# Transposing by row halves of the array, and scores on its four quarters, in a fused Mamba and local-attention kernel

## The reference

```python
def local_attention(q, k, v):            # 8 heads of 64, windows of 64
    bq = q.reshape(b, h, w, WINDOW, d) * QK_SCALE
    ...                                  # keys and values: the window before and the own one
    sim = jnp.einsum('bhwid,bhwjd->bhwij', bq, bk)
    mask = (i < j) | (i > j + WINDOW) | (j == -1)
    sim = jnp.where(mask, -jnp.finfo(sim.dtype).max, sim)
    attn = jax.nn.softmax(sim, axis=-1)
    out = jnp.einsum('bhwij,bhwjd->bhwid', attn, bv)
```

## Time and profile before

| | |
|---|---|
| median of 3 runs | 1633.24 us (1629.99 to 1635.3) |
| the profiled execution's own time | 1627.94 us |
| its span, from first to last instruction | 1626.2 us |
| mean clock granted to TensorE, as a share of 2.4 GHz | 0.872 |
| PE busy | 1266.1 us, 8096 matmuls |
| PE weight loads busy (PEld) | 761.9 us, 8096 loads |
| DVE busy | 1111.9 us |
| ACT busy | 756.7 us |
| POOL busy | 729.8 us |

### The profile page before, as it was taken

The page is one execution under the profiler, slowest core; times in us unless marked ns, Lnnn a source line. Parts: engine busy times, 40 slices in busy tenths (PEclk is TensorE's granted clock), DMA queues, the critical chain, the costliest instruction groups (busy, mean ns, idle before and its releaser), DMA issues. The chain is left out here.

```text
span 1626.2 us, 22154 instructions
## 1 busy us (share of the span) xinstructions
PE 1266.1 (78%) x8096; PEld 761.9 (47%) x8096; DVE 1111.9 (68%) x1700; ACT 756.7 (47%) x1832; POOL 729.8 (45%) x357
## 2 busy tenths in 40 slices
PE   2867867887869888788879878798797878768685
PEld 0223433454545545445455545455464546455353
DVE  6859856968768667787686678686676755563442
ACT  1644525535545284443635365443655444444251
POOL 0007404655355634663455445464445545552351
PEclk8878978998989899888999889897998979889787
DMA  4000000000000000000000000000000000000000
GB/s 157 0 7 1 1 7 0 1 1 7 1 7 7 2 7 1 7 7 7 1 1 8 7 7 1 7 8 0 1 1 1 7 1 1 1 7 1 7 1 7
DMA packets 14317, 12.54 MB, mean 8 GB/s; under 512 B 1093, under 2 KB 12543, under 8 KB 14207
## 3 DMA queue, kind: packets, MB, share of 16 engines
q1 hardware_dynamic: 14207, 11.10, 2.2%
HBM read 9.00 MB, written 2.10 MB: 7 GB/s over the span
## 5 line engine op out<-in xcount | busy, mean ns | idle before, releaser
L805 DVE TENSOR_TENSOR_SCAN scan<-du,decay 128x1028 f32<-128x1028 f32 x128 | 392.0, 3079 | 68.6 <-ACT decay L593 68.5
L499 POOL TENSOR_TENSOR rn<-ssc,expo 128x16 f32<-128x16 f32 x64 | 186.1, 2908 | 457.2 <-DVE ssc L866 457.0
L995 PE MATMUL Y<-scan,diag 128*128 128x512 f32 x512 | 277.1, 669 | 77.6 <-DVE scan L805 77.6
L647 ACT ACTIVATE prob<-B,nmax 128x128 f32<-128x128 f32 x512 | 180.3, 377 | 326.6 <-DVE nmax L901 326.5
L519 POOL TENSOR_TENSOR qk<-qk,rn 128x1024 f32<-128x1024 f32 x64 | 199.2, 3113 | 5.0
L995 PEld LDWEIGHTS Y<-scan,diag 128*128 128x128 f32 x512 | 97.4, 210 | 186.8 <-DVE scan L805 107.4
L593 ACT ACTIVATE decay<-delta,negA 128x1024 f32<-128x1024 f32 x128 | 146.2, 1163 | 34.6 <-DVE scan L805 34.5
L610 ACT ACTIVATE sq<-A 128x512 f32<-128x512 f32 x128 | 74.6, 601 | 182.4 <-PE A L995 182.3
L515 POOL TENSOR_TENSOR qk<-qc,qs 128x1024 f32<-128x1024 f32 x64 | 153.8, 2404 | 2.5
L995 PE MATMUL B<-kT,qT 64*64 64x128 f32 x2048 | 151.4, 291 | 0.0
L995 PEld LDWEIGHTS B<-kT,qT 64*64 64x64 f32 x2048 | 117.9, 141 | 50.6 <-issue 50.6
(11 more groups left out here) (141 smaller groups left out, 2309.1 us busy)
## 6 DMA issues: line engine op xcount, KB each, us to landing
xT<-in_xT SPq DMA_DIRECT2D x8, 256.0 KB, 2.6
x<-in_x SPq DMA_DIRECT2D x8, 256.0 KB, 3.1
out<-outb SPq DMA_DIRECT2D x8, 256.0 KB, 2.3
wqkv<-in_wqkv SPq DMA_DIRECT2D x1, 1536.0 KB
w<-in_w SPq DMA_DIRECT2D x1, 682.0 KB
wo<-in_wo SPq DMA_DIRECT2D x1, 512.0 KB
bv<-in_bv SPq DMA_DIRECT2D x1, 328.0 KB, 3.9
rope_c<-in_rope_c SPq DMA_DIRECT2D x2, 128.0 KB
```

The source lines that it names most:

```text
L499: pool.tensor_tensor(rn[:, :], ssc[:, :], expo[:, 0:2 * HEADS], ALU.pow).then_inc(rn_sb, 1)
L647: ins = act.activation(prob[:, h, :], B[a][:, c * P:(c + 1) * P], ACT.Exp, bias=nmax[:, q % 2, h:h + 1], accum_out=den[:, q % 2, h:h + 1])
L805: dve.tensor_tensor_scan(state, step, a, 0.0, ALU.add, ALU.mult).then_inc(scan_sb, 1)
L995: return pe.matmul(dst, lhsT, rhs, start=start, stop=stop, skip_group_check=True)
```

## The change

Each of the three steps is laid out anew.

- Transposes work on 64 rows at a time: row half `w` (window `w`'s queries, or positions) has all 128 columns as its stationary operand and is moved through by a 64x64 piece of the identity, so that each transpose writes 64 columns. Row half 0 writes to `B[0]`, row half 1 to `B[1]`. There are 16 of them where there were 8, the two halves by turns, and both banks signal only at the end. `probs_T` therefore waits for the probabilities of all heads first, and `qk_T` for both copies of `probT`.
- `probT` is now laid out by window, and q and k lie together in one buffer, `qkT`, for one sequence instead of two. ACT still makes two copies of 128x512 for it, but each takes q and k of one window. The wait for the scores of the tile before (`s_ps`) stands where it was, ahead of the first copy.
- `scores` puts the mask in by four matmuls of 64 rows and 64 columns, one for each quarter of the array (row half `a`: even or odd heads; column half `w`: the window), and then goes through the pairs of heads with the four quarters by turns. Both signals come at the very end.

```diff
             def probs_T(q):
-                for a in range(2):
-                    pe.wait_ge(prob_sb, 2 * q + a + 1)
-                    for c in range(PAIRS):
-                        ins = pe.transpose(B[a][:, c * P:(c + 1) * P], prob[:, 2 * c + a, :], ident[:, :])
-                    ins.then_inc(pT_ps, 1)
+                pe.wait_ge(prob_sb, 2 * q + 2)
+                for h in range(HEADS):
+                    for w in range(2):
+                        ins = pe.transpose(B[w][:, h * WIN:(h + 1) * WIN], prob[half(w), h, :], ident[half(w), half(w)])
+                        if h == HEADS - 1:
+                            ins.then_inc(pT_ps, 1)
 
             def qk_T(q):
                 pe.wait_ge(qk_sb, q + 1)
                 done = before("qk_T", (q,), "probs_T")
-                for a in range(2):
-                    if done:
-                        pe.wait_ge((pTe_sb, pTo_sb)[a], done)
-                    for c in range(PAIRS):
-                        ins = pe.transpose(B[a][:, c * P:(c + 1) * P], qk[:, a, c * P:(c + 1) * P], ident[:, :])
-                    ins.then_inc(qkT_ps, 1)
+                if done:
+                    pe.wait_ge(pTe_sb, done)
+                    pe.wait_ge(pTo_sb, done)
+                for at in range(2 * PAIRS):
+                    for w in range(2):
+                        ins = pe.transpose(B[w][:, at * WIN:(at + 1) * WIN],
+                                           qk[half(w), at // PAIRS, at % PAIRS * P:(at % PAIRS + 1) * P],
+                                           ident[half(w), half(w)])
+                        if at == 2 * PAIRS - 1:
+                            ins.then_inc(qkT_ps, 1)
...
                 pe.wait_ge(qkT_sb, 2 * q + 2)
-                for a in range(2):
-                    rows = slice(a * DH, (a + 1) * DH)
-                    mm(B[a][:, :], identb[:, :],
-                       mask[:, j, :].unsqueeze(1).to_broadcast((P, PAIRS, P)), True, False)
-                    for c in range(PAIRS):
-                        for wd in range(2):
-                            lo = j * P + wd * WIN
-                            keys = kT[rows, s, c, lo:lo + 2 * WIN]
-                            if wd == 0:
+                for w in range(2):
+                    for a in range(2):
+                        mm(B[a][half(w), :], identb[half(a), half(a)],
+                           mask[half(a), j, w, :].unsqueeze(1).to_broadcast((WIN, PAIRS, P)), True, False)
+                for c in range(PAIRS):
+                    for w in range(2):
+                        lo = j * P + w * WIN
+                        for a in range(2):
+                            keys = qkT[half(a), 1, c, lo:lo + 2 * WIN]
+                            if w == 0:
                                 keys = keys.rearrange("p (b x) -> p b x", b=2)[:, ::-1, :]
-                            ins = mm(B[a][wd * WIN:(wd + 1) * WIN, c * P:(c + 1) * P],
-                                     qT[rows, c, wd * WIN:(wd + 1) * WIN], keys, False, c == PAIRS - 1)
-                    ins.then_inc(s_ps, 1)
+                            ins = mm(B[a][half(w), c * P:(c + 1) * P],
+                                     qkT[half(a), 0, c, WIN + lo:2 * WIN + lo], keys, False, c == PAIRS - 1)
+                            if c == PAIRS - 1 and w == 1:
+                                ins.then_inc(s_ps, 1)
```

More of the change, by code:

```diff
@@ L220, in build @@
         carry = sb("carry", [P, P])
-        mask = sb("mask", [P, 2, P], BF16)
+        mask = sb("mask", [P, 2, 2, P], BF16)
         rope_c = sb("rope_c", [P, LAYERS, 2, 2, DH])
@@ L276, in build @@
         prob = sb("prob", [P, HEADS, P])
-        probT = sb("probT", [P, HEADS, P])
+        probT = sb("probT", [P, 2, HEADS, WIN])
         o_s = sb("o_s", [P, INNER])
@@ L449, in _ @@
                 load_x(g)
-            for dst, src in [(prob[:, 0:2, :], t["mask"]), (rope_c[:, 0], t["rope_c"]), (rope_s[:, 0], t["rope_s"]),
+            for dst, src in [(prob[:, 0:4, :], t["mask"]), (rope_c[:, 0], t["rope_c"]), (rope_s[:, 0], t["rope_s"]),
                              (rope_c[:, 1], t["rope_c"]), (rope_s[:, 1], t["rope_s"]),
@@ L615, in probs_T @@
                     act.wait_ge(o_ps, q)
-                act.activation(probT[:, 1::2, :], B[1][:, :].rearrange("p (h x) -> p h x", x=P),
-                               ACT.Copy).then_inc(pTo_sb, 1)
+                act.activation(probT[:, 1], heads(B[1][:, :]), ACT.Copy).then_inc(pTo_sb, 1)
             def v_in(q):
@@ L628, in qk_T @@
                 l, g, i = TILE[q]
-                s, j = i // 2, i % 2
-                act.wait_ge(qkT_ps, 2 * q + 1)
                 if q:
                     act.wait_ge(s_ps, 2 * q)
[L633 to L636, removed]
+                for r in range(2):
+                    act.wait_ge(qkT_ps, 2 * q + r + 1)
+                    lo = WIN + i % 2 * P + r * WIN
+                    act.activation(qkT[:, :, :, lo:lo + WIN],
+                                   B[r][:, :].rearrange("p (a c x) -> p a c x", a=2, c=PAIRS), ACT.Copy).then_inc(qkT_sb, 1)
             def softmax(q):
@@ L693, in _ @@
             dve.memset(hT[:, :, :, 0:1], 0.0)
[L694 removed]
+            dve.memset(qkT[:, :, :, 0:WIN], 0.0)
             dve.memset(v_even[:, :, :], 0.0).then_inc(zeros_ready, 1)
@@ L732, in _ @@
             once(dve.tensor_copy(identb[:, :], ident[:, :]))
-            once(dve.tensor_copy(mask[:, :, :], prob[:, 0:2, :]))
+            once(dve.tensor_copy(mask[:, :, :, :].rearrange("p j w x -> p (j w) x"), prob[:, 0:4, :]))
             for l in range(LAYERS):
@@ L881, in probs_T @@
                     dve.wait_ge(o_ps, q)
-                dve.tensor_copy(probT[:, 0::2, :], B[0][:, :].rearrange("p (h x) -> p h x", x=P)).then_inc(pTe_sb, 1)
+                dve.tensor_copy(probT[:, 0], heads(B[0][:, :])).then_inc(pTe_sb, 1)
             def weighted(q):
@@ L1233, in _consts @@
     own, before = j <= i, j >= i
[L1234 to L1237, removed]
+    mask = np.zeros((2, 2, WIN, P), bool)
+    mask[0, 0] = np.concatenate([own, np.zeros_like(before)], 1)
+    mask[1, 0] = np.concatenate([own, before], 1)
+    mask[:, 1] = np.concatenate([before, own], 1)
+    mask = np.tile(mask.transpose(2, 0, 1, 3).reshape(WIN, 4, P), (2, 1, 1))
     eye = np.eye(P, dtype=np.float32)
```

9 lines of the change are left out of this document (5 added, 4 removed).

## The result

The changed kernel takes 1676.28 us, median of 4 runs (1671.79 to 1678.28), against 1632.20 of the kernel before beside it (1629.99 to 1635.30): ratio 1.0265, 95% interval 1.0236 to 1.0293. It is 44 us slower; the forecast was 8 us faster.

What follows compares the result with a forecast made beforehand. PE and DVE wait for each other by turns, with PE's later half mostly off the path. Turns -8, outside -3 and -3, clock +6 sum to -8 us: 1633.24 to 1625, range 1598 to 1650.

Steps and rivals of the forecast that it cites:

- the prices: Time PE saves a tile: 1.25 us in scores, 0.22 in probs_T, 0.31 in qk_T, in all 1.8.
- row halves by turns: Rival, scores and transposes: row halves don't overlap, scores save nothing, DVE's copy starts later; 1652 us or more, chance 0.08.
- slow transposes: Rival, probs_T and qk_T: transposes gain nothing at the 0.107 us pace; 1641 us, chance 0.23 together with the clock's.
- clock rival: Slot 2's state_y falls to half clock behind a longer wait: +3.3 us a turn, 1648; chance 0.23 together with slow transposes.
- the forecast's own two terms: Savings of qk_T (0.31 us) and scores (1.25), taken to lengthen the wait ahead of slot 2's state_y.
- The clock: Step on slot 2's state_y: half clock behind a longer wait costs 1.8 us a turn; half was counted, +6 us.
- Terms of 0.2 to 0.6 us a turn: Gains on a turn's loops: slots 2 and 6 0.44, slot 6 0.6, slot 3 0.2, slot 7 0.3.
- the gain of 1.1 to 1.2 us a turn: Net of gains and losses on the loops of a turn; 6.5 turns make -8 us.
- Lost: 4 x 0.1 = 0.4: Slots 1, 3, 4, 5: DVE's copy starts 0.76 us after the first transpose instead of 0.64, losing 0.4 a turn.
- outside of the turns, -3 and -3: Last tile's chain through scores and qk_T at half clock, -3 us; the 12 tiles before it, -3.
- the signs named: Checks: PE's scan waits grow by some 50 us, DVE's probT wait stays near 71.7; wrong if turns change over 2.
- The main reading: PE's work from v_in to out_T lies beside DVE's, so the change cheapens a half that mostly isn't waited for.

Runs made afterwards that it cites:

- e17: The kernel before with two useless maxima in DVE's work of one tile in each turn, about 1.2 us more: 1623.07 us.
- e18: The kernel before with four useless maxima in DVE's work of one tile in each turn, about 2.4 us more: 1638.16 us.
- e2: The changed kernel with the masks and scores of before, so only the transposes are changed: 1629.86 us.
- e12: The changed kernel with useless matmuls at three places: eight behind out_T, sixteen ahead of norm_T, eight ahead of u_in: 1621.60 us.
- e9: The kernel before, where only the transposes wait for both banks and report both at once; scores report as before: 1646.55 us.
- e14: The kernel before with waits and reports as late as in the changed one, plus useless matmuls at three places: 1645.28 us.
- e15: The kernel before with only the transposes changed to row halves, plus useless matmuls at three places: 1622.60 us.
- e3: The changed kernel with its masks written seven times over, without changing any value: 1650.74 us.
- e6: The kernel before with eight useless matmuls behind out_T of every tile but the last three: 1615.39 us.
- e11: The kernel before with useless matmuls at three places: eight behind out_T, sixteen ahead of norm_T, eight ahead of u_in: 1617.37 us.
- e5: The changed kernel with eight useless matmuls behind out_T of every tile but the last three: 1635.42 us.
- e16: The changed kernel with more useless matmuls at three places: twelve behind out_T, twenty-four ahead of norm_T, twelve ahead of u_in: 1660.49 us.
- e10: The kernel before with only masks and scores changed to quarters, plus eight useless matmuls behind out_T: 1634.90 us.
- e4: The kernel before with only its waits and signals as in the changed one, all reports late: 1658.25 us.
- e7: The kernel before, where only the scores' first bank is reported late, when the second is done too: 1642.24 us.
- e13: The kernel before with only masks and scores changed to quarters, plus useless matmuls at three places: 1628.68 us.
- e1: The kernel before with only masks and scores changed to quarters, transposes as before: 1659.24 us.

## Why the prediction was wrong

**Right: the prices.** Row halves and column halves run side by side: the 32 product records start four at a time, every 0.109 us (0.98 in all up to `out_T`; 0.87 forecast), `scores` takes 1.22 us (1.4 forecast), the transposes' load is the short one (143 ns), sixteen take 0.64 with the change of shape (0.5 to 0.6 forecast). The rivals on row halves by turns and on slow transposes are out. The place of the clock rival was right too: the wait at 1015.20 passed 3.10 us and `state_y` went from 1.82 to 3.58. The wait grew by 0.8 us only and not by up to 1.7 (the forecast's own two terms make 1.6): 0.57 of what was saved stands as a wait ahead of the `state_y` before it.

**Wrong: the step called "The clock".** "I put half of 1.8 into the sum, 6.5 x 0.9 = +6." The mechanism was in the forecast, but at one place of the turn, with half its weight, and as a term that adds. The change costs 44 us without fill, 20 with fill at one place in both kernels and 4 with fill at three, so most of the loss came through PE's waits and the clock behind them; how much exactly stays open, since useless work moves more than the clock and the turns go in steps. The rival that has this mechanism gave +3.3 us a turn, 1648. The turn grew by 6.8. By the starts of `weighted`, slot 2 to 3 has +0.5, 6 to 7 +0.9, 7 to 0 +1.8, 0 to 1 +0.6, and 1 to 2 +2.8; the last is where the rival had 3, and it had 1.5 at one more place, but took off a gain of 1.2 that did not come and had nothing at the rest. What each of these slots lost through the clock was not measured apart.

**Wrong: the form of the sum.** Terms of 0.2 to 0.6 us a turn were multiplied by 6.5 and added. In e17 1.2 us on DVE's path cost nothing in the mean of the turns, and in e18 2.4 us cost 1.6. So a term far below 3.4 us a turn could not be priced by its own length, and the gain of 1.1 to 1.2 us a turn did not come: e2 has faster transposes and the turn of before, e12 has the whole change, at full clock behind slot 2's wait, and the turn of before.

**Wrong in the same way: "Lost: 4 x 0.1 = 0.4"** for the later copy. Its start was right (0.75). What a later report costs depends on which step it makes the turn take: one step, 3.4 us, for slow matmuls (e9, e14), none for the changed ones (e2, e12, e15).

**Wrong: outside of the turns, -3 and -3.** Ahead of the four middle turns the changed kernel lost 14.3 us and behind them 8.0. `scores` did get shorter at half clock as well (2.28 us at 1590.02, 4.91 before), but nothing of it shows in the time, and where the 14.3 and the 8.0 us were lost was not followed.

Of the signs named, PE's wait for scans grew by 29 us, not 50, and DVE's wait for `probT` did not stay near 71.7 but rose to 97.6. The turn changed by more than 2 us, which the forecast had named as the sign that it is wrong. The main reading, that PE's later half of a slot is mostly not waited for, held. It was the reason for most of the loss as well: work that nobody waited for had kept the clock up, as e3 shows by putting such work back.

**A better version.** e6 and e11, the kernel before with fill, take 0.9908 of its time without (0.9882 to 0.9934), and beat both kernels. In e11 the four middle turns take 752.3 us, as before (751.0), and what lies behind them 406 instead of 421: the gain is in the last part, where PE's chains have no scans beside them. The changed kernel with fill (e12) beats both too, by less.

## What to carry to other kernels

Before making an engine's work shorter, ask what it does in that time otherwise. Where TensorE waits a few us between bursts, shorter bursts lengthen waits, and the half clock behind a wait can cost more than the burst saved; work without use in the wait shows in one run whether a loss comes this way (e3, e5), and roughly how much of it. Too much of it costs more than the clock gives back (e16 against e12). And where a loop keeps the same length to a tenth of a us turn after turn, look for steps before adding up tenths.

## What the runs showed of the hardware

- A loop of 187.7 us mostly changed its length in steps of 3.4 us: turns of 187.7, 191.1 and 194.6, 184.6 once, or two turns that sum to whole steps. It was so in 15 of the 20 kernels; in e6 and e10, and in part of the turns of e4, e11 and e14, it was not (e6 had 185.6 and 187.1). That the turns keep step with the clock's changes is argued from e7 and e18, where the long turns are those with `state_y` at half clock; no run here took the clock's changes away, and e13 has the longer turn with this `state_y` at full clock.
- The length of the wait alone did not decide the clock behind it. Ahead of slot 2's `state_y`, a wait of 3.42 or 3.43 us was always followed by half clock (3.57 us for the step, e1 and changed), and 2.63 to 2.67 always by full clock in the kernel before (1.82). But in e18 waits of 2.65 to 2.67 us were followed by 1.82 and by 3.29 to 3.41 us by turns, in e3 2.97 by 1.82 and 3.31, and a wait of 2.54 by 1.82 us at full clock in all turns of e12 and by 2.21, with `attn_out` slow behind it (4.83), in all turns of e5. The Trainium skill, TensorE: Matmul & The Clock Gate, "Part 1: The HAM clock gate", says that the chip judges TensorE's activity in a rhythm of its own that doesn't start with the kernel. That the same wait is followed by either clock agrees with it.
- Useless work made the kernel faster by 0.9% on TensorE (e6), and by 0.65% on VectorE, ahead of a scan that TensorE waits for (e17).
- Four quarters of the array start four 64x128 float32 products every 0.109 us (e1 and changed); two column halves start two in the same time.
